# An expert feedforward as one chain of 88 slots with fp32r parts, and its weights split inside the cross attention before it

## The reference

```python
# cross attention
scores = where(mask, x @ ctx.T / sqrt(512), -1e30)
out = softmax(scores) @ ctx                       # zero where a batch has no valid token

# expert feedforward, DFF 1408, E 8 experts of rank R 16, top K 2
gate, up = x @ Wg.T, x @ Wu.T
base = silu(gate) * up @ Wd.T
w = softmax(x @ Wr.T), kept at its two largest entries
for e in range(8):
    h = silu(gate + 2 * x @ Ag[e].T @ Bg[e].T) * (up + 2 * x @ Au[e].T @ Bu[e].T)
    acc += 2 * (h @ Ad[e].T @ Bd[e].T) * w[:, e]
out = base + acc
```

## Time and profile before

| | us |
|---|---|
| median of 3 runs | 2614.13 (2604.57 to 2614.92) |
| profiled execution, device time | 2613.25 |
| its span, first to last instruction | 2611.5 |

### The profile page before, as it was taken

One profiled execution on the slowest core, in us unless ns is written; L12 is line 12 of the kernel. 1 busy time (PEld: TensorE's weight loads), 2 busy tenths in 40 slices (PEclk: granted clock), 3 DMA queues, 4 the chain that ended last, 5 costly groups with the idle time before them and its releaser, 6 DMA issues. The chain is left out here.

```text
span 2611.5 us, 32892 instructions
## 1 busy us (share of the span) xinstructions
PE 1969.5 (75%) x11984; PEld 1450.6 (56%) x11984; DVE 1357.5 (52%) x2704; ACT 741.0 (28%) x1233; POOL 450.7 (17%) x470
## 2 busy tenths in 40 slices
PE   3258888323665999999999995999968996267766
PEld 2135555222434777777877784787846774133333
DVE  8657766486554232222322314566554776456666
ACT  1015555100211221121121112222214002565565
POOL 0122321000000000000000001010103765023334
PEclk9859998656876999999999997999988998588887
DMA  4099995312534000000000003000013114500000
GB/s 177 21 139 153 145 158 85 113 36 83 175 112 162 1 17 18 1 17 18 1 17 17 9 1 113 17 33 17 17 44 137 43 41 152 202 8 25 24 17 24
DMA packets 111911, 169.17 MB, mean 65 GB/s; under 512 B 9104, under 2 KB 65040, under 8 KB 109328
## 3 DMA queue, kind: packets, MB, share of 16 engines
q1 hardware_dynamic: 102672, 150.35, 23.2%
q10 hardware_dynamic: 9088, 16.78, 1.7%
HBM read 120.70 MB, written 46.14 MB: 64 GB/s over the span
## 5 line engine op out<-in xcount | busy, mean ns | idle before, releaser
L1317 DVE TENSOR_TENSOR f_hid<-f_gate,f_gu 128x256 f32<-128x256 f32 x264 | 111.1, 421 | 437.5 <-ACT f_gate L1229 434.3
L1229 ACT ACTIVATE f_gate<-f_gu 128x256 f32<-128x256 f32 x264 | 100.6, 383 | 485.9 <-PE f_gu L1140 352.1
L453 DVE TENSOR_REDUCE a_rowmax<-a_ring 128x2 f32<-128x512 f32 x256 | 165.0, 687 | 100.6 <-PE a_ring L532 98.5
L1974 PE MATMUL e_py<-e_kv,e_toep 128*128 128x320 f32 x640 | 179.1, 435 | 0.0
L1152 PE MATMUL f_gu<-f_low,f_bg 128*128 128x256 f32 x704 | 168.1, 380 | 6.5 <-DVE f_hid L1317 6.5
L1166 PE MATMUL f_pout<-f_wd,f_hid 128*128 128x512 f32 x352 | 165.4, 592 | 0.0
L1140 PE MATMUL f_gu<-f_xhi,f_wg 128*128 128x256 f32 x704 | 152.1, 314 | 4.1 <-issue 4.1
L405 ACT ACTIVATE a_prob<-a_sT 128x1024 f32<-128x1024 f32 x128 | 130.6, 1026 | 81.8 <-PE a_sT L521 81.7
L1974 PEld LDWEIGHTS e_py<-e_kv,e_toep 128*128 128x128 f32 x640 | 119.2, 190 | 45.7
L1152 PEld LDWEIGHTS f_gu<-f_low,f_bg 128*128 128x128 f32 x704 | 127.9, 190 | 28.4 <-issue 10.5
L1140 PE MATMUL f_gu<-f_xhi,f_wu 128*128 128x256 f32 x704 | 133.4, 288 | 0.0
(11 more groups left out here) (348 smaller groups left out, 4416.1 us busy)
## 6 DMA issues: line engine op xcount, KB each, us to landing
a_qs<-parts SPq DMA_DIRECT2D x96, 128.0 KB, 6.6
a_ks<-parts SPq DMA_DIRECT2D x96, 128.0 KB, 7.0
parts<-a_hi SPq DMA_DIRECT2D x16, 512.0 KB, 8.7
parts<-a_lo SPq DMA_DIRECT2D x16, 512.0 KB, 8.7
e_toep<-in_taps SPq DMA_DIRECT2D x32, 256.0 KB
a_xf<-in_xT SPq DMA_DIRECT2D x1, 4096.0 KB, 21.1
ctxT<-a_turned SPq DMA_DIRECT2D x16, 256.0 KB, 9.6
a_cf<-ctxT SPq DMA_DIRECT2D x1, 4096.0 KB, 13.1
```

The costliest lines, as they stand in the source:

```text
L453: dve.tensor_reduce(rowmax[:, s % 2, :, e * SLOTS + j], ring[n % RING][:, :].rearrange("p (q t) -> p q t", t=T), AX.X, ALU.max, negate=Tru ...
L1229: act.activation(gate[:, (u * H + n) % 2, :], gu[f % 4][:, 0, :], ACT.Silu).then_inc(gate_ready, 1)
L1317: dve.tensor_tensor(hid[:, f % 4, j, :], gate[:, (u * H + n) % 2, :], gu[f % 4][:, 1, :], ALU.mult).then_inc(hid_ready, 1)
L1974: last = pe.matmul(py[n % RING][:, 0:DIAG * BS], toep[:, h % 3, (t - j) * P:(t - j + 1) * P], kv[:, h % 2, j, :], start=(j == 0), stop=(j ...
```

## The change

Cross attention: the hardware loop goes; 16 tiles are one chain written out, with three buffers for the batches' data, six for tiles of x and four for results. Each tile is stored as soon as it is normalised. The masks are made batch by batch. Beside that 35 pieces of the feedforward's weights (`PIECES`: 2 of `Ag`/`Au`, 11 of `Wd`, 4 of `Bg`/`Bu`, 2 of `Ad`, 16 halves of `Wg` and `Wu`) are loaded by SyncE into five buffers `c_raw`, two or three in each of the 16 slots; ScalarE copies the high part, VectorE subtracts for the low part. The 15 pieces of `Wd`, `Bg` and `Bu` (`SENT`) go through two buffers `c_sent` and are written to the scratch tensors `wds` and `bgs`. The others stay in SBUF for the next stage.

Expert feedforward: 88 slots t (8 batches of 11 tiles) are one chain without a loop; forms 1 and 2 of tile n come in slots n+1 and n+2 whatever the batch, so that the tiles of the next batch follow without a drain. `wd` and `bg` stream from `wds` and `bgs` in three and four buffers, one tile each per slot. The expansion with `bg`, the products with `ad` and with `wd` are three fp32r products each instead of one fp32 product; for that ScalarE copies the three hidden tiles (`hh`, 128 x 768) and VectorE subtracts (`hl`) once a slot, and the masked low rank values are split by ScalarE (`lowh`) and GpSimd (`lowl`). x has three buffers, loaded from ScalarE's queue. The product with `bd` goes through `misc` in slots 5 and 6 of the next batch. The diff, cut to its core:

```diff
 def cross_attention(nc, io, sem, keep):
-    TILES = 2 * TB
+    NT = N // P
+    XT, CT, RAW, HALF = 6, 3, 5, DFF // 2
+    def pieces_of(s):
+        return [n for n in range(NP) if n * NT // NP == s]
 # SyncE
+                def load_x(b):
+                    if b >= CT:
+                        sp.wait_ge(s_["added"], TB * (b - CT + 1))
 ...
+                def load_piece(n):
+                    kind, a, c = PIECES[n]
+                    if n >= RAW:
+                        sp.wait_ge(s_["w_low"], n - RAW + 1)
 ...
+                def send_piece(n):
+                    sp.wait_ge(s_["w_low"], n + 1)
 ...
+                load_x(0)
+                load_x(1)
+                load_x(2)
+                for n in range(RAW):
+                    load_piece(n)
+                for s in range(NT):
+                    if s % 2 == 0 and CT <= s // 2 + 1 < B:
+                        load_x(s // 2 + 1)
+                    for n in pieces_of(s):
+                        if n in SENT:
+                            send_piece(n)
+                        if n + RAW < NP:
+                            load_piece(n + RAW)
 # ScalarE, end of a slot
+                        for n in pieces_of(s):
+                            act.wait_ge(piece_in[n % RAW], 16 * (n // RAW + 1))
+                            if n in SENT and SENT.index(n) >= 2:
+                                i = SENT.index(n)
+                                act.wait_ge(piece_out[i % 2], 32 * (i // 2))
+                            act.activation(parts(n)[0], staged(n), ACT.Copy).then_inc(s_["w_high"], 1)
 # VectorE, end of a slot
+                        for n in pieces_of(s):
+                            dve.wait_ge(s_["w_high"], n + 1)
+                            dve.tensor_tensor(parts(n)[1], staged(n), parts(n)[0], ALU.subtract).then_inc(s_["w_low"], 1)

 def expert_feedforward(nc, io, sem, keep):
+    NS = B * FT
+    WR, BR, XT = 3, 4, 3
 # SyncE
+                for n in range(NS):
+                    if n >= BR:
+                        sp.wait_ge(gu_done[2], n - BR + 1)
+                    sp.dma_start(bg[:, n % BR, :, :, :].bitcast(F32), io["bgs"][n % FT]).then_inc(got_bg[n % BR], 16)
+                    if n >= WR:
+                        sp.wait_ge(s_["taken"], n - WR + 1)
+                    sp.dma_start(wd[:, n % WR, :, :].bitcast(F32), io["wds"][n % FT]).then_inc(got_wd[n % WR], 16)
 # TensorE
+                def expand(n, j):
 ...
+                    for w in range(2):
+                        for h, xs in ((0, lowh), (0, lowl), (1, lowh)):
+                            last = pe.matmul(gu[n % 3][:, w, :], bg[:, n % BR, h, w, :], xs[:, u, j - 1, w, :],
+                                             start=False, stop=True, skip_group_check=True)
+                def down(t):
+                    pe.wait_ge(s_["hl_ready"], t + 1)
 ...
+                            for m, (ws, xs) in enumerate(((ad[0], hh), (ad[0], hl), (ad[1], hh))):
 ...
+                            for m, (xs, h) in enumerate(((hh, 0), (hh, 1), (hl, 0))):
+                                last = pe.matmul(pout[q][:, :], xs[:, t % 2, 0, cols], wd[:, n % WR, h, :],
 ...
+                turn_x(0, 0)
+                turn_x(0, 1)
+                logits(0)
+                base(0)
+                turn_logits(0)
+                base(1)
+                base(2)
+                turn_masks(0, 0)
+                turn_masks(0, 1)
+                low_rank(0)
+                for t in range(1, NS + 3):
+                    b, s = t // FT, t % FT
+                    ahead, tail = b + 1 < B, 1 <= b <= B
+                    if 0 <= t - 2 < NS:
+                        expand(t - 2, 2)
+                    if t - 1 < NS:
+                        expand(t - 1, 1)
+                    if ahead and s == 8:
+                        turn_masks(b + 1, 0)
+                    if 3 <= t < NS:
+                        base(t)
+                    if ahead and s in (1, 2):
+                        turn_x(b + 1, s - 1)
+                    if ahead and s == 3:
+                        logits(b + 1)
+                    if ahead and s == 4:
+                        turn_logits(b + 1)
+                    if tail and t < NS and s in (5, 6):
+                        back(b - 1, s - 5)
+                    if ahead and s == 8:
+                        turn_masks(b + 1, 1)
+                    if ahead and s == 9:
+                        low_rank(b + 1)
+                    if t - 1 < NS + 2:
+                        down(t - 1)
 # ScalarE, end of a slot
+                        act.activation(hh[:, t % 2, lo:hi, :], hid[:, lo:hi, :], ACT.Copy).then_inc(s_["hh_ready"], 1)
 ...
+                    if b >= 1 and s == 0 and XT <= b + 1 < B:
+                        load_x(b + 1)
 # VectorE, start of a slot
+                    dve.tensor_tensor(hl[:, t % 2, lo:hi, :], hid[:, lo:hi, :], hh[:, t % 2, lo:hi, :], ALU.subtract
+                                      ).then_inc(s_["hl_ready"], 1)
```

More of the change, by code:

```diff
@@ L1176, in _ @@
[L1176 to L1186 removed]
+                    last.then_inc(s_["a_done"], 1)
@@ L1235, in _, with load_x, store_x @@
-                for s in range(1, 9):
-                    ahead(s, (0, 0))
-                batches(act, slots)
-                for u in range(2):
-                    act.wait_ge(stored[u], 16 * (B // 2 + 1))
+                def load_x(b):
+                    if b >= XT:
+                        act.wait_ge(stored[b % XT], 16 * (b // XT))
+                    act.dma_start(xt[:, b % XT, :, :], rows("x2", b)).then_inc(got_x[b % XT], 16)
+                def store_x(b):
+                    act.wait_ge(s_["x_ready"], (b + 1) * TB)
+                    act.dma_start(rows("x3", b), xt[:, b % XT, :, :]).then_inc(stored[b % XT], 16)
@@ L1365, in _ @@
-                batches(dve, slots)
+                    dve.memset(rankv[:, :, e], float(E_ - e)).then_inc(s_["rank_made"], 1)
+                dve.wait_ge(s_["rank_made"], E_)
+                x_high(0)
+                route_start(0)
+                route_normal(0)
+                route_choose(0)
+                route_choose(1)
+                route_weigh()
+                grow(0)
+                low_product(0)
+                for t in range(NS + 3):
+                    b, s = t // FT, t % FT
+                    ahead, tail = b + 1 < B, b >= 1
+                    if 0 <= t - 1 < NS + 2:
+                        hidden_low(t - 1)
+                    for j in (2, 1):
+                        if 0 <= t - j < NS:
+                            hidden(t, j)
+                    if tail and s == 1:
+                        take_base(b - 1)
+                    if tail and s == 2:
+                        take_one(b - 1)
+                    if ahead and s == 4:
+                        x_high(b + 1)
+                    if ahead and s == 5:
+                        route_start(b + 1)
+                    if ahead and s == 6:
+                        route_normal(b + 1)
+                        route_choose(0)
+                    if ahead and s == 7:
+                        route_choose(1)
+                        route_weigh()
+                    if tail and t < NS and s == 8:
+                        normal(b - 1)
+                    if ahead and s == 10:
+                        low_product(b + 1)
+                    if t < NS:
+                        hidden(t, 0)
+                    if tail and t < NS and s == 3:
+                        take_two(b - 1)
+                    if tail and t < NS and s in (5, 6):
+                        take_back(b - 1, s - 5)
+                    if ahead and s == 7:
+                        grow(b + 1)
@@ L1368 @@
+                take_two(B - 1)
+                for q in range(TB):
+                    take_back(B - 1, q)
+                normal(B - 1)
 STAGES.append(expert_feedforward)
```

962 lines of the change are left out of this document (496 added, 466 removed).

## The result

The kernel after takes 2492.89 us (median of 4 runs, 2491.03 to 2498.77), the kernel before beside it 2611.04 (4 runs): a ratio of 0.9554, 95% interval 0.9526 to 0.9582. The forecast was 2512, with a range of 2478 to 2560. The profiled execution took 2498.77 us with a span of 2497.0.

| stage, us | before | after | change | forecast |
|---|---|---|---|---|
| cross attention | 123.1 | 143.7 | +20.6 | +22 (8 to 50) |
| expert feedforward | 810.2 | 667.5 | -142.7 | -124 (-137 to -105) |
| all else, code unchanged | 1678.2 | 1685.8 | +7.6 | 0 |

What follows compares the result with a forecast made beforehand. Stages run one after another; TensorE bounds the feedforward loop, DMA and VectorE its preparation. 2613.3 us minus 124 (feedforward) plus 22 (cross attention) gave 2511, with the median's 0.9 offset 2512; range 2478 to 2560.

Steps and rivals of the forecast that it cites:

- The slot: Feedforward chain: one slot's TensorE products take 6.39 us against 7.15, 67 us less over 88 slots.
- rival (c): Feedforward: fp32r products at half an fp32 pass, weight loads hidden, a slot of 5.83 us, -49, 2463; chance 3%.
- The stalls of the boundaries: Feedforward loop before: 8.1 us lost at each of six batch boundaries, waits for x then half pace; stalls about 50.
- The stage's length: Expert feedforward: 686 us against 810.2, 124 us less (105 to 137).
- Stalls of 8: Feedforward: 1 us for late x on each of five batches and 3 us for all else (0 to 30).
- Drain of 6: Feedforward's end: two slots of drain without cover cost 6 us.
- The load of x at a boundary: Feedforward from batch 2 on: x load issued about 2 us after base(0), needed at 6.4; 1 us each on five batches.
- The cross attention: Whole stage: 145 us against 123, 22 more (8 to 50); VectorE at 6.8 us a slot in slots 8 to 15.
- Rival (a): Cross attention bound by written-piece hand-over and queues: slots 1 to 7 11 us, 8 to 15 7.5; +33, 2545; chance 15%.
- (b): Cross attention: TensorE falls to half clock, 8.5 us of work a slot instead of 6.8, +25, 2537; chance 5%.
- (d): Feedforward: scratch stream of `wd` and `bg` sets the slot; slower than before, about 2680 at 95 GB/s; chance 3%.
- (e): Feedforward chain: an engine late at each boundary keeps the 50 us of stalls in another form, 2554; chance 6%.

Runs made afterwards that it cites:

- e1: The kernel after with expansions and products with `ad` and `wd` as one fp32 product of the high parts instead of three fp32r products: 2559.1 us.
- b1: The kernel before with three buffers instead of two for x of the expert feedforward, its loop over batches written out: 2571.0 us.
- e2: The kernel after with three buffers instead of two for the weight pieces written back to HBM: 2491.8 us.
- v1: The kernel after with written and kept weight pieces alternating, pieces from slot 2, a batch's loads on own semaphores, transposed context loaded earlier: 2470.7 us.
- v3: The kernel after with v1's changes, a changed feedforward start, and cross attention x in four buffers, x and transposed context loaded earlier: 2466.7 us.

## Why the prediction was right, and where it was wrong

- **The slot**: 6.39 forecast, 6.37 measured; -67 forecast, -68.2 measured by e1. The price 0.1187 of a product held for the new ones. The gap formula of the Trainium skill ("TensorE: Matmul & The Clock Gate", section Back-to-back issue gap) would have had 0.109 and 0.216: 0.117 and 0.237 were measured, and rival (c), whose time the formula would nearly give, is out.
- **The stalls of the boundaries**: "about 50". b1 takes 42.4 away, 23.0 of wait, 12.9 of half clock and some 4 of the hardware loop's rounds among it, and leaves 1.0 at each boundary. The mechanism, wait and half clock together, was read rightly from rows 4. But "the hardware loops become straight code: nothing" put at nothing a term that the trace of the kernel before shows: two waits, 4.1 us.
- **The stage's length** is where the forecast failed: 686 against 667.5. Taken apart: base(3) at 42.5 instead of 45.5 (3.0 less, of it 1.2 the earlier landing of x, at 4.3 us; TensorE's idle 5 us ahead of the first expansion were 4.95). Stalls of 8 for late loads of x and all else: none. Drain of 6: one wait of 1.8 (4.2 less), for the two slots of drain still cover each other with expansions and products. TensorE's work from base(3) to the end of the last product with `ad` (1449.56) took 610.3 us without that wait, where the forecast has 615 less the last closing pair, 613.3 (3.0 less): each of seven batches takes 79.25 (from the Silu at 1284.26 to that at 1363.51, eleven slots on) and not 79.8. From there to the end of the stage, closing pair included, 12.8 instead of 11.5 + 1.7 = 13.2 (0.4 less). 3.0 + 8 + 4.2 + 3.0 + 0.4 = 18.6, the 18.5 but for rounding. The one step that failed by much is "stalls 8 (0 to 30)", a reserve put beside slack of 3.4 us that had been worked out and was there.
- **The load of x at a boundary**, "the one tight place": issued behind the copy of slot 0, it landed in 4.5 us (median of eight) and nobody waited.
- **The cross attention**: +20.6 for +22, for partly wrong reasons, and so by luck. Slots 8 to 15 were to be VectorE's at 6.8 us. VectorE needs 5.8 to 6; the ring of x's buffers sets about 7 (49.6 us for the seven slots between the scores of tiles 7 and 14). The step that failed: the loads of x were priced by bandwidth alone, never as a ring with a landing time. And VectorE's work on a tile was put too high, in part because it was read from start to start of the last tiles of a pair (2.8 us, rows 10), of which VectorE is idle 0.3. Two errors met in one number. Slots 1 to 7 were rightly said to hang on writes, in slot 5 most of all: 12.3 us between the scores of tiles 4 and 5 (695.02 to 707.33), the longest slot, with three written pieces, and with a wait for x of 7.0 beside them.
- **Rival (a)** had slots 1 to 7 at 11 us each; they took 7.6. **(b)**: the clock did fall, to 0.79 in slots 1 to 7 and 0.88 in slots 8 to 15, but TensorE was busy 33.8 of 52.9 and 41.2 of 56.3 us there and set no pace. **(d)** and **(e)** did not happen.

## What to carry to other kernels

A buffer that comes free only when a later stage of the pipeline is done makes a ring: issue, landing, the pipeline's depth, release. Work out its length in slots beside every engine's busy time; here one more buffer of x gave some 38 us in one stage of the kernel before (42.4 with its loop written out), and in another stage the missing one hid behind a forecast that came out right. Check a forecast that hits by its parts' reasons and not by its sum alone. And of changes that relieve the same queue, price them together: three that gave 13 us one by one gave 24 at once.

## What the runs showed of the hardware

- The DMA share of a window is no sign of the limit: 0.96 at 315 GB/s in the kernel after, 1.02 at 342 in e2, 1.05 at 379 in v1 and v3, with the same kinds of transfers in another order.
- A stream of 1280 KB a slot beside TensorE at 100% changed no product's pace (a batch takes 79.25 us with it and without, TensorE busy 587.09 of 588.00). The landing of `wd` grew by 0.5 us, that of `bg` fell from 3.3 to 2.7.
- At the start of the chain, after 5.0 us idle, TensorE's expansions follow each other by 0.21 us at a granted clock of 0.50, and from 831.14 on by 0.12 at 1.00. The same at the six boundaries of the kernel before, behind waits of 3.4 to 4.0 us for x, cost 2.1 us each on top of the wait. TensorE's products of the kernel after there:

```profile
826.93 0.58 PE L1243 MATMUL f_gu<-f_lowh,f_bg 128*128 128x256 f32 x1 [4.95 <-POOL f_lowl L1149]
827.31 0.41 PE L1243 MATMUL f_gu<-f_lowl,f_bg 128*128 128x256 f32 x1
827.52 0.63 PE L1243 MATMUL f_gu<-f_lowh,f_bg 128*128 128x256 f32 x2
...
831.14 0.28 PE L1243 MATMUL f_gu<-f_lowh,f_bg 128*128 128x256 f32 x1
831.26 0.28 PE L1243 MATMUL f_gu<-f_lowl,f_bg 128*128 128x256 f32 x1
831.38 0.40 PE L1243 MATMUL f_gu<-f_lowh,f_bg 128*128 128x256 f32 x2
```
